# Ten identity matmuls per batch placed in the waits behind the two Gelus

## The reference, cut to what matters

```python
x = x + attn0(norm(x)) + experts(norm(x))        # layer 0
xn = norm(x)                                     # layer 1
h = silu(xn @ w1.T * s1) * (xn @ w2.T * s2)      # 128 -> 512
h = gelu(h @ h1.T * hs1, approximate=False)      # 512 -> 512, first Gelu
h = gelu(h @ h2.T * hs2, approximate=False)      # 512 -> 512, second Gelu
x = x + attn1(xn) + h @ w3.T * s3                # 512 -> 128
```

## Time and profile before

| | |
|---|---|
| median of 3 runs | 1833.97 us (1833.51 to 1834.12) |
| the profiled execution's own time | 1832.24 us |
| its span | 1830.3 us, 33215 instructions |
| TensorE matmul busy | 1637.3 us (89%) |
| VectorE busy | 1213.7 us (66%) |
| ScalarE busy | 1170.3 us (64%) |
| GpSimd busy | 836.0 us (46%) |
| mean granted TensorE clock | 0.944 |

### The profile page before, as it was taken

How to read it: one execution, slowest core, us unless ns; L and a number is a source line. 1 busy time by engine, 2 the same in 40 slices (tenths; PEclk the granted TensorE clock), 3 DMA queues, 4 the chain that set the end, 5 groups by cost and what they waited for, 6 DMA issues and landing times.

```text
span 1830.3 us, 33215 instructions
## 1 busy us (share of the span) xinstructions
PE 1637.3 (89%) x12146; PEld 700.0 (38%) x12146; DVE 1213.7 (66%) x3101; ACT 1170.3 (64%) x2226; POOL 836.0 (46%) x736
## 2 busy tenths in 40 slices
PE   3786899899999999999999999999989999988876
PEld 1353453245323543345333553345423543322321
DVE  6545578557875688656875588656876578576632
ACT  2682866587557865677656875687656875635542
POOL 3453654265435653455434644356534643423142
PEclk9997999999999999999999999999999999989985
DMA  5001200101110101101101101101101101010010
GB/s 214 30 24 35 59 20 15 56 8 36 50 38 24 36 25 47 41 13 36 50 21 36 42 25 36 53 13 36 45 27 36 37 18 30 30 41 18 18 35 6
DMA packets 63681, 66.79 MB, mean 36 GB/s; under 512 B 8144, under 2 KB 58144, under 8 KB 62624
## 3 DMA queue, kind: packets, MB, share of 16 engines
q1 hardware_dynamic: 63520, 64.68, 11.7%
HBM read 40.73 MB, written 23.59 MB: 35 GB/s over the span
## 4 chain that ended last, share of the span: by engine, by line
PE 66%; DVE 13%; ACT 10%; issue 6%; POOL 3%; DMA 1%; SPq 0%; POOLq 0%; ACTq 0%; DVEq 0%
PE banks L376 65%; DVE negmax L744 6%; ACT probs L1021 3%; ACT hm L1081 2%; ACT h_hi L1082 2%; POOL h_lo L1237 1%; ACT L1021 1%; DVE h L907 1%; DVE r_b L932 1%; DVE pack L751 1%; ACT h L1118 1%; POOL h_lo L1185 1%; DVE xn L765 1%; PE banks L601 1%; DVE xs L844 1%
## 5 line engine op out<-in xcount | busy, mean ns | idle before, releaser
L1021 ACT ACTIVATE probs<-banks 128x512 f32<-128x512 f32 (+3 forms) x1216 | 580.5, 533 | 360.7 <-PE banks L376 350.8
L744 DVE TENSOR_REDUCE negmax<-banks 128x1 f16<-128x512 f32 x768 | 493.2, 687 | 143.1 <-PE banks L376 139.2
L1185 POOL TENSOR_TENSOR h_lo<-hm,h_hi 128x512 f16<-128x512 f32 x256 | 296.4, 1159 | 310.1 <-ACT h_hi L1082 309.4
L740 DVE CUSTOM_DVE_ANT_0 scr<-banks,mask_row 128x384 bf16<-128x384 f32 (+3 forms) x512 | 230.5, 488 | 225.2 <-PE banks L376 223.0
L376 PE MATMUL banks<-kp,qs 32*128 32x512 f16 (+3 forms) x1024 | 234.4, 361 | 47.2 <-DMA kp<-relk 22.5
L376 PE MATMUL banks<-probs,vp 128*32 128x512 f32 (+3 forms) x2048 | 247.7, 558 | 0.0
L1081 ACT ACTIVATE hm<-banks,cols 128x512 f32<-128x512 f32 x256 | 176.8, 690 | 99.7 <-PE banks L376 97.9
L376 PE MATMUL banks<-qs,kp 32*128 32x512 f16 (+3 forms) x1024 | 204.0, 358 | 40.7 <-ACT probs L1021 37.8
L1196 POOL TENSOR_TENSOR psums<-psums,probs 128x1024 f32<-128x1024 f32 x64 | 149.0, 2356 | 130.6 <-PE banks L376 130.6
L376 PE MATMUL banks<-w_hi,h_hi 128*128 128x128 f16 x1152 | 204.9, 220 | 1.2 <-POOL h_lo L1237 1.2
L376 PE MATMUL banks<-w_lo,h_hi 128*128 128x128 f16 x1152 | 204.4, 220 | 0.0
(11 more groups left out here) (166 smaller groups left out, 2447.2 us busy)
## 6 DMA issues: line engine op xcount, KB each, us to landing
qkc<-relm SPq DMA_DIRECT2D x96, 128.0 KB, 3.2
qs<-relq SPq DMA_DIRECT2D x64, 128.0 KB, 2.1
kp<-relk SPq DMA_DIRECT2D x64, 128.0 KB, 2.2
relm<-halves SPq DMA_DIRECT2D x32, 256.0 KB, 2.1
relq<-halves SPq DMA_DIRECT2D x16, 256.0 KB, 2.1
relk<-halves SPq DMA_DIRECT2D x16, 256.0 KB, 2.3
h<-split_in SPq DMA_DIRECT2D x3, 1024.0 KB, 5.6
xs<-x_in SPq DMA_DIRECT2D x8, 256.0 KB, 3.3
```

Of the source, the lines that this page charges most:

```text
L740: v.tensor_tensor_reduce(scr[:, s, 0:kw], psum[:, SCO + s, 0:kw], mask_row[:, T - kw:T], -1.0, 3e38, ALU.add, ALU.min, negmax[:, g.n % 2, ...
L744: v.tensor_reduce(negmax[:, g.n % 2, c, h:h + 1], psum[:, SCO + s, 0:kw], AX.X, ALU.max, negate=True).then_inc(sem("max"), 1)
L1021: a.activation(keys(g, c)[:, 2 * pair + s, q0:T], psum[:, TRA + s, q0:T], ACT.Exp, scale=SCALE[main(g)]).then_inc(sem("exp"), 1)
L1185: p_.tensor_tensor(out=h_lo[:, (e + 1) % 2, hc, :], in0=hm[:, i % 2, :], in1=h_hi[:, (e + 1) % 2, hc, :], op=ALU.subtract).then_inc(sem("h ...
```

## The change

`TURNS = (6, 4)` and two new entries in the slot table are added: `turn 0` at slot 72 and `turn 1` at slot 87 of a batch, which are the slots behind the first and the second Gelu of the batch before. A new function `turn_over` is called on TensorE between `score` and `trans`. In those slots, if the slot has a score unit, TensorE waits until VectorE has reduced the first of the two tiles just computed, and then multiplies the fp16 identity by itself, repeated four times to 512 columns, 6 times behind the first Gelu and 4 times behind the second, into the PSUM bank that was just reduced. Nobody reads the result; the next `score` overwrites it. No other engine gets or loses an instruction.

Slot 72 has a score unit in batches 1 to 7, slot 87 in batches 0 to 6. That makes 14 places and 7 x 6 + 7 x 4 = 70 matmuls. Slot 87 of batch 0 (slot 87 of the whole program) has no Gelu before it. The second Gelu of batch 6 and both Gelus of batch 7 get no matmuls.

```diff
+TURNS = (6, 4)
...
+AT.update({("turn", k): at for k, at in enumerate((72, 87), 0)})
...
+                def turn_over(G):
+                    u = UNIT.get(G)
+                    for k, many in enumerate(TURNS):
+                        if u is not None and due(G, ("turn", k)) is not None:
+                            g, j = u
+                            pe.wait_ge(sem("max"), 2 * (8 * g.n + j) + 1)
+                            for _ in range(many):
+                                mm(SCO, slice(0, T), ident16[:, :], ident16[:, :].unsqueeze(1).broadcast_to([P, NC, P]), True, True)
...
                     if G in UNIT:
                         score(*UNIT[G])
+                    turn_over(G)
                     if G in TRANS:
                         trans(*TRANS[G])
```

## The result

| | before | after |
|---|---|---|
| median of 5 runs | 1833.97 us (1831.85 to 1835.53) | 1823.62 us (1820.71 to 1824.40) |
| profiled execution | 1832.24 us, span 1830.3 | 1824.04 us, span 1822.1 |
| mean granted clock | 0.944 | 0.951 |

The ratio of after to before is 0.9943, with a 95% interval of 0.9932 to 0.9954: 10 us faster, where I had forecast 21 us. In the changed kernel `mm` is L378, the reductions are L752 and L756, the Gelu is L1130.

A forecast was written before the change was run, and what follows sets the result against it. TensorE, busy 89% of the span, was taken as the bound, with idle gaps and half clock behind Gelus. Gain 23.4 less 2.5 us added is 20.9 us: 1811.3 us profiled, 1813 us predicted, range 1803 to 1829.

The forecast's parts named there:

- first Gelus, batches 0 to 6: Half-clock stretches behind seven first Gelus go: 7 x 1.2 + 2 x 0.89 = 10.2 us gained.
- second Gelus, batches 1 to 5: Half-clock stretches behind these five second Gelus go, at 1.2 us per first part and 1.21 per second: 10.8 us gained.
- All four pieces: TensorE idle time left around the new matmuls: about 0.6 and 0.3 us behind first Gelus, 0.7 and 0.6 behind second.
- all 13 falls: Half-clock stretches behind first Gelus of batches 0 to 6 and second of 0 to 5, 68.32 us together; gain 23.4 us.
- Rival 1: Four matmuls behind the second Gelu are too few; gain 7.7 us, 1826 us; chance 0.16.
- two gaps of rows 8: TensorE gaps of 1.95 us, followed by half clock, and 1.29 us, where the clock stayed at 1.00.
- first parts: The first 3.42 us of each half-clock stretch; removing one was taken to gain 1.2 us.
- second part: The rest of a 6.83 us half-clock stretch after 3.42 us: 0.89 us behind first Gelus, 1.21 behind second.
- uncovered places: Slots 167 and 87, where no wait hides the matmuls: costs 1.0 us (0 to 2.1) and 1.5 us (0 to 2.5).
- rival 2: The falls move: the 1.29 us gap might join, six new falls at 1.2 us; 1820 us; chance 0.07.
- Rival 3: Identity matmuls do not count, all 13 falls stay; 1836.5 us, at most 1838.6; chance 0.10.
- rival 4: The matmuls come at half clock and push the path, with no fall avoided; costs 10 to 12 us, 1845 us; chance 0.05.

The follow-up runs named there:

- e6_three_first: Changed kernel with three identity matmuls behind each first Gelu instead of six, and nothing elsewhere; 1833.7 us, 1.0003 of before.
- e2_first_only: Changed kernel with only the six matmuls behind the first Gelus, neither wait nor matmuls in the other seven places; 1821.8 us, 0.9941 of before.
- e5_wait_only: Changed kernel with its waits in all 14 places but no matmuls behind them; 1837.0 us, 1.0017 of before.
- e8_all_gaps: Changed kernel with six behind second Gelus, none at slots 87 and 167, and batch 6's second, batch 7's Gelu gaps and the 1.95 us gaps filled; 1801.8 us.
- e1_six_six: Changed kernel with six identity matmuls behind the second Gelu too, instead of four; 1820.2 us, 0.9929 of before.
- e11_again: The changed kernel with no edit, traced a third time; 1817.58 us.
- e3: Changed kernel with only the four matmuls behind the second Gelus and at slot 87; 1826.5 us, 0.9962 of before.
- e9: As e6_three_first, but with a hidden-layer weight matrix as both operands in place of the identity; 1836.5 us, 1.0006 of before.

## Why the prediction was wrong

The profiled execution gained 8.2 us where its own sum said 20.9. By the prediction's terms, from the stages of both traces:

| term | predicted | measured |
|---|---|---|
| first Gelus, batches 0 to 6 | +10.2 | +10.0 |
| second Gelus, batches 1 to 5 | +10.8 | +7.7 |
| second Gelu of batch 0, its uncovered place taken off | +2.4 - 1.0 | -2.4 |
| slot 87 | -1.5 | -2.3 |
| all the rest | 0 | -4.8 |
| sum | 20.9 | 8.2 |

The sum of the trace is 12.7 us short: 3.1 behind the second Gelus of batches 1 to 5, 3.8 behind batch 0's, 0.8 at slot 87, 0.2 behind the first Gelus, and 4.8 in stages that the prediction put at nothing.

**The step that failed** is "All four pieces are far below 1.29 us. I therefore take it that all 13 falls go." Behind second Gelus they did not: four of five stayed in the first trace, and e6_three_first showed that pieces of 0.67 and 0.78 us can be followed by a fall. The length of one piece is not what counts. Rival 1, four are too few, was right in substance and wrong in being yes or no: four held in one, three and all five of the five places in three traces of the same program, and six held in all 15 of three others. (The two gaps of rows 8, against which the pieces were measured, are batch 3's and not of "the same batch", 2; nothing hangs on it.)

The trace of before already spoke against the step. Ahead of the fall behind batch 0's second Gelu, one of the 13, TensorE had no gap like the others, only short pieces:

```profile
366.33 0.39 PE L376 MATMUL banks<-kp,qs 32*128 32x512 f16 x1 [0.55 <-DVE negmax L740]
366.94 0.38 PE L376 MATMUL banks<-kp,qs 32*128 32x512 f16 x1 [0.23 <-DVE negmax L740]
...
368.42 0.21 PE L376 MATMUL banks<-kp,qs 32*128 32x128 f16 x1 [0.24 <-DVE negmax L740]
368.95 0.23 PE L376 MATMUL banks<-kp,qs 32*128 32x128 f16 x1 [0.31 <-DVE negmax L740]
369.58 0.91 PE L376 MATMUL banks<-qs,kp 32*128 32x512 f16 x2 [0.41 <-ACT probs L1021]
```
```profile
370.29:377.12 6.83, 6.10 (x28) 0.50 0.00 0
```

None is longer than 0.55 us, and the clock fell. The prediction counted this fall among the 13 that go (2.4 us), though it said itself that `trans` does not wait there; it stayed in every trace, with four matmuls, with six and with none.

**The prices** were good for first parts (1.2 taken, 1.15 and 1.43 measured) and low for a second part behind a second Gelu (1.21 taken, 1.50 measured in one batch). The 7.7 us of the second term are mostly one first part and the second parts; but by e2_first_only three of the four second parts would have gone without the four matmuls. That the term came out at 7.7 of 10.8 is therefore in part luck.

**The uncovered places** were found, but sized at the middle of their bounds: the stage with slot 167 got 2.4 us longer, over the upper end of 2.1, and with the wait and no matmul 2.0 (e5_wait_only), a longer half-clock stretch included. The 2.3 us at slot 87 is one pair of traces in a stage that varies by as much from trace to trace.

**The rest**, 4.8 us that the sum put at nothing, is rival 2, falls that move, with the wrong gap named: the 1.29 us gap brought none in the first trace. In that trace 3.4 us were gained ahead of first Gelus and 1.1 behind batch 6's second, and lost were 3.6 and 1.1 behind batch 7's two Gelus, 2.9 at a new stretch of 6.83 us between the end of batch 5's branch and batch 6's first tanh, and 1.7 in the same stage one batch later. The loss behind batch 7's first Gelu (40.6 to 40.8 us where before has 37.2) stands in all nine traces in which batch 6's first Gelu kept its clock and batch 7's gap was not filled; filled, in e8_all_gaps, it turns into a gain. Why the clock came back so late there stays open.

Rival 3 and rival 4 are out: the identity counts, and the matmuls came at full clock in every covered place of all traces.

## What to carry to other kernels

Where an engine's clock depends on its work, look first for gaps that end in a half-clock stretch, and price a stretch by the same stage with one part more and one part less. Filling such a gap with idle work pays if the filling is nearly the whole of it: three matmuls were worth nothing, four held the clock in 17 of 25 places, six every time. Don't take a single gap that kept the clock as proof that shorter pieces will. Put it only where the engine would wait anyway: of 14 places two had no cover, and by the stages of the first trace they took back 4.7 us, about a quarter of the 17.7 that the covered ones gave.

## What the runs showed of the hardware

The same program had four, two and no falls of the clock in the same five places in three executions, and their times are 1824.0, 1821.3 and 1817.6 us. A single profile is therefore not the program's pattern.

An identity and a dense weight matrix as operands did the same to the clock: 6 and 5 falls in seven places with three matmuls.

A granted clock of 1.00 shown for the first 70 us of a trace need not be true. Windows of e1_six_six and, behind it, of e11_again say 0.50 and 1.00 for the same stretch:

```profile
23.08:70.86 47.78, 23.77 (x85) 0.50 0.25 83
```
```profile
23.08:70.86 47.78, 23.76 (x86) 1.00 0.25 83
```

But TensorE's timelines in that stretch are alike, e1_six_six first:

```profile
60.66 0.63 PE L378 MATMUL banks<-xl,w_hi 128*128 128x512 f16 x1
61.09 0.63 PE L378 MATMUL banks<-xh,w_lo 128*128 128x512 f16 x1
```
```profile
61.69 0.63 PE L378 MATMUL banks<-xl,w_hi 128*128 128x512 f16 x1
62.11 0.63 PE L378 MATMUL banks<-xh,w_lo 128*128 128x512 f16 x1
```

One matmul of 512 columns follows the last by 0.42 to 0.43 us in both (60.66 to 61.09, 61.69 to 62.11), which is the step at half clock; at full clock it is 0.22 us (rows 8). So both executions ran at half clock there; the records of the clock begin at 69.6 us in e11_again's trace and at 19.7 in e1_six_six's, and before them the view shows 1.00. In all 13 traces of this case the step is 0.42 or 0.43 us from 50 to 67 us. Four of them (e1, e3, e6, e9) show that as 0.50 and the others as 1.00, which makes 47.8 / 2 / 1817 = 0.013 of difference in the mean granted clock with no difference in time. The 0.944 and 0.951 of before and after both lack it and can be compared.
